# Eight loads at the end of a routed two-layer kernel: all at once, or two in flight

## The reference

```
x = x + gnn(layernorm(x), adj)
    agg = epsilon * x + adj @ x
    h   = silu(rmsnorm(agg @ W1 + b1) * rms_weight)      # 128 -> 512
    out = h @ W2 + b2                                    # 512 -> 128
x = x + ffn(layernorm(x))
    scores = x @ Wg.T + bg          # 8 experts, the best 2 per token
    p = softmax(top 2 scores)
    out = sum over the 2 experts of p * (relu(x @ W1[e].T + b1[e]) @ W2[e].T + b2[e])
```

## Time and profile before

| | |
|---|---|
| median of 3 runs | 562.39 us (561.38 to 563.0) |
| the profiled execution's own time | 561.8 us |
| its span | 560.0 us |
| TensorE busy | 531.0 us, 95% |
| VectorE, ScalarE, GpSimd busy | 64%, 53%, 73% |
| queue of SyncE (q1) | 104.08 MB, 51.1% of 16 engines' span |
| mean over the span | 219 GB/s |
| mean granted TensorE clock | 0.99 |

### The profile page before, as it was taken

The page is one execution under the profiler, slowest core; times in us unless marked ns, Lnnn a source line. Parts: engine busy times, 40 slices in busy tenths (PEclk is TensorE's granted clock), DMA queues, the critical chain, the costliest instruction groups (busy, mean ns, idle before and its releaser), DMA issues.

```text
span 560.0 us, 13703 instructions
## 1 busy us (share of the span) xinstructions
PE 531.0 (95%) x3642; PEld 440.8 (79%) x3642; DVE 357.9 (64%) x1202; ACT 296.5 (53%) x779; POOL 411.5 (73%) x671
## 2 busy tenths in 40 slices
PE   2999999999999999999999999999999999999982
PEld 1477766676666777567799999999999999999950
DVE  2558696886978969868867456654454444444483
ACT  3455654547645465554665455555555555555520
POOL 5423878788887878878877587888888766677770
PEclk9999999999999999999999999999999999999995
DMA  8998334553445543364165465677775747766998
GB/s 278 421 422 330 95 137 168 196 188 119 131 162 194 188 161 106 132 255 152 39 223 193 167 226 200 231 243 267 263 249 193 278 169 262 257 221 233 333 314 343
DMA packets 40203, 122.42 MB, mean 219 GB/s; under 512 B 7967, under 2 KB 18976, under 8 KB 37824
## 3 DMA queue, kind: packets, MB, share of 16 engines
q1 hardware_dynamic: 30768, 104.08, 51.1%
q0 software_dynamic: 8640, 16.93, 9.0%
q10 hardware_dynamic: 720, 0.54, 0.3%
HBM read 61.19 MB, written 24.02 MB: 152 GB/s over the span
## 4 chain that ended last, share of the span: by engine, by line
PE 63%; POOL 15%; issue 7%; DMA 5%; DVE 4%; ACT 4%; SPq 0%; DVEq 0%; POOLq 0%; ACTq 0%
PE ps_y L699 14%; PE ps_agg L589 8%; POOL slots L977 7%; PE ps_g L699 7%; PE ps_y L563 6%; POOL x_all L970 3%; PE ps_agg L668 3%; PE ps_h L668 3%; PE ps_h L672 3%; PE ps_agg L669 3%; PE ps_h L669 3%; PE ps_agg L672 3%; PE ps_t L576 3%; ACT hn L765 2%; PE ps_t L527 2%
## 5 line engine op out<-in xcount | busy, mean ns | idle before, releaser
L1045 POOL DMA_INDIRECT parts<-adj_in x142 | 141.5, 996 | 58.5 <-ACT adj_in L880 31.7
L977 POOL DMA_INDIRECT slots<-rows,dest x128 | 131.3, 1025 | 22.5 <-issue 22.0
L589 PE MATMUL ps_agg<-adj_in,xn_both 128*128 128x512 f32 x256 | 128.3, 610 | 10.1 <-DVE adj_in L1109 10.1
L880 ACT ACTIVATE adj_in<-adj_in,share 128x128 f32<-128x128 f32 x142 | 49.4, 395 | 101.1 <-issue 89.2
L699 PE MATMUL ps_y<-W2e,adj_in 128*128 x768 | 93.9, 275 | 0.0
L699 PEld LDWEIGHTS ps_y<-W2e,adj_in 128*128 128x128 f32 x768 | 89.9, 192 | 0.0
L1295 DVE TENSOR_TENSOR xe_split<-ps_t,xe_split 128x256 fp32r<-128x256 f32 x71 | 30.0, 424 | 80.3 <-ACT xe_split L828 74.8
L589 PEld LDWEIGHTS ps_agg<-adj_in,xn_both 128*128 128x128 f32 x256 | 45.1, 195 | 34.0 <-issue 31.1
L563 PEld LDWEIGHTS ps_y<-consts,siluT 128*128 128x128 f32 x480 | 57.0, 192 | 7.2 <-issue 7.2
L765 ACT ACTIVATE hn<-hb 128x512 f32<-128x512 f32 x64 | 39.7, 621 | 39.8 <-DVE hb L1115 39.8
L563 PE MATMUL ps_y<-consts,siluT 128*128 128x128 f32 x480 | 58.9, 277 | 0.0
(11 more groups left out here) (199 smaller groups left out, 1127.4 us busy)
## 6 DMA issues: line engine op xcount, KB each, us to landing
wcur<-expert_w SPq DMA_DIRECT2D x71, 512.0 KB
adj_in<-in_adjT SPq DMA_DIRECT2D x15, 2048.0 KB, 8.8
adj_in<-slots SPq DMA_DIRECT2D x71, 130.0 KB
expert_w<-parts SPq DMA_DIRECT2D x8, 512.0 KB, 5.2
out<-x_all SPq DMA_DIRECT2D x8, 512.0 KB, 8.0
x_all<-in_x SPq DMA_DIRECT2D x1, 3072.0 KB, 17.8
parts<-adj_in POOLq DMA_INDIRECT x142
adj_in<-in_adjT SPq DMA_DIRECT2D x2, 1024.0 KB, 7.6
```

Source lines behind the costliest of these rows:

```text
L589: ins = pe.matmul(ps_agg[par][:, :], xn[b % 2][:, m, :], adj_in[par][:, m, :], start=(m == 0), stop=(m == TPB - 1))
L880: ins = act.activation(ye[ku][:, j, :], yb[ku % 2][:, j, :], ACT.Copy, scale=share[ku][:, j:j + 1])
L977: pool.indirect_dma_start(out=slots, out_offset=bass.IndirectOffsetOnAxis(ap=dest[q % 2][:, c, j:j + 1], axis=0), in_=rows[q % 2][:, c, j, ...
L1045: pool.indirect_dma_start(out=parts, out_offset=bass.IndirectOffsetOnAxis(ap=goes[u % 8][:, j, :], axis=0), in_=ye[ku][:, j, :], in_offset ...
```

## The change

Before each low load from the third on, SyncE waits until the load two before has landed. The number of loads, their sizes, their destinations and their order are the same, and so is everything else in the kernel.

```
     GFIRST, FIRST = 11, 8
     EARLY = (2 * GTOK * GE - E * (TILE - 1)) // TILE
     BOTH_PAIRS = 24
+    IN_FLIGHT = 2
     CH = 8
...
             results_landed(counts[0])
             for n in range(NCH):
+                if n >= IN_FLIGHT:
+                    sp.wait_ge(s_low[n - IN_FLIGHT], 16)
                 sp.dma_start(low_part_in[n], parts_t[:, 0, n * CH:(n + 1) * CH, :]).then_inc(s_low[n], 16)
             for k in range(4):
                 sp.wait_ge(s_W1cur[k], 16 * ((NTILE + 3 - k) // 4))
```

## The result

The changed kernel takes 564.31 us (median of 16, 562.89 to 567.09); the kernel before, beside it, 561.63 (16 runs, 560.28 to 564.28). The ratio is 1.0047, with a 95% interval of 1.0032 to 1.0061: slower by 2.6 us. The forecast was 562.6, a change too small to be told from none; the range to 565.0 holds the time, but what came is the slower rival, which had a chance of 0.17.

A forecast was written before the change was run, and what follows sets the result against it. The bound was a chain of waits through the last scatter to high 4 to 7, with crowded transfers second. 0 us at a 3.7 us load, 0.2 at 3.8, put as +0.2: 562.6 on the median's scale, range 561.1 to 565.0.

The forecast's parts named there:

- slower rival: Low loads' round trips outlast SyncE's cover: +1.7 us at 4.3 us a load, +4.7 at 5.3; chance 0.17.
- odd chain 1, 3, 5, 7: SyncE's low loads: each odd one issues when the previous odd one lands; low 7 issues at 533.9, lands at 537.6.
- slack of 540:543: DMA engines at share 0.71, 185 GB/s before the change; high 3's 1.4 us of lateness was to fall into it.
- bytes of 527:533: DMA during throttled low loads: share forecast near 0.68 instead of 1.02.
- signs of being wrong: Low loads over 4 us, high 4 landing past 545 or issued past 541, or TensorE idle before 535.
- how long a load takes with at most one other ahead: Low loads two in flight: 3.7 us taken, between high 0's 3.6 and high 4's 3.8.
- rival's own rule: Three latencies chained to low 7: each 0.1 us on a load puts 0.3 us on high 3.
- low pair's 4.3 and 6.3: Latencies of low 0 and low 1 before the change, median 5.3; long latencies were called a queue, not a transfer's price.
- faster rival: Scatters land sooner in a lighter queue, so high 4 lands 1.3 us sooner: 561.1; chance 0.11.
- last gate: SyncE's wait before high 4 for the scatter issued at 534.45; taken to open at 540.4, unchanged by the edit.
- 1.6 us to spare: Low 7 was to land at 537.6, ahead of TensorE's start on its chunk at 539.16.
- 8.4 us of cover: SyncE's idle wait for scatters before high 0, until 533.53, meant to hide the added waits.

The follow-up runs named there:

- placebo: Changed kernel with its six waits moved to the expert biases' semaphore, long full, so none waits; ratio 1.000 (0.9981 to 1.0019) to the kernel before.

## Why the prediction was right or wrong

The place was right: the odd chain 1, 3, 5, 7 sets when SyncE is free, high 0 to 3 stand behind low 7, and high 4 lands right behind them. Right too: readers of the low parts of chunks 0 to 6 do not wait, the slack of 540:543 is filled, the bytes of 527:533 fell to 0.69 of 417 GB/s (forecast as a share, 0.68; the share itself read 0.93), and the waits as instructions cost nothing (placebo, 1.000). The prediction's signs of being wrong came, as it named them: low loads over 4 us, and high 4 landing past 545, at 519.9 + 27.0 = 546.9 on its clock.

The step that failed is "how long a load takes with at most one other ahead", 3.7 us. Counted from low 0:

| | forecast | changed kernel |
|---|---|---|
| low 1 lands | +6.6 | +5.8 |
| low 3 lands | +10.3 | +11.8 |
| low 5 lands | +14.0 | +15.9 |
| low 7 lands | +17.7 | +20.5 |
| high 0 issued | +14.5 | +16.5 |
| high 3 lands | +22.9 | +25.8 |
| high 4 lands | +24.3 | +27.0 |
| end of span | +40.3 | +42.1 |

Low 3, 5 and 7 took 6.0, 4.1 and 4.6 us, 14.7 for three against 11.1. Their 3.6 us, less the 0.8 by which low 1 came sooner, are the 2.8 us by which low 7 landed later than forecast. Every row below carries it on: 2.9 at high 3, 2.7 at high 4, 1.8 at the end. The rival's own rule, 0.3 us on high 3 for each 0.1 us on a load, held. At a mean of 4.9 and with low 1 as measured it gives high 3 at +5.8 + 14.7 + 5.2 = +25.7.

That the time lies inside the range is partly luck. The range held a load up to 4.6 us. For 4.9 the rival's rule gives +3.5 us, or 565.9 on the median's scale, and 564.3 came because two things outside the sum were favourable: low 1 landed 0.8 us sooner (0.2 and 0.6 in the two other profiles), and the stretch from high 4 to high 7 was shorter than before, as shown below.

Why 3.7 was the wrong row: high 0 and high 4 were each the first of a batch behind little or nothing. A load in a running pair always has a partner, and halving the bytes of both took 1.7 us off a round trip, not the 0.63 us that half a load is worth alone. The lower of the two rows was also a low reading: in three other profiles with the old ending high 0 took 3.9, 4.1 and 4.6 us, while high 4 took 3.8 or 3.9 each time. No row before has two loads in flight and nothing behind them. The low pair's 4.3 and 6.3 are nearest for the start, though six more loads stood behind them; I called their excess a queue and left 5.3 out of the range. The fit of the Trainium skill (DMA: Bandwidth & Descriptors, Anatomy of one DMA), 3.2 us, is further off still. The page gives it for a DMA that GpSimd issues, and has no term for others in flight; here no low load of full size took less than 3.5 us, even alone.

From the low loads alone the end should have moved by high 4's 2.6 us (+24.4 to +27.0). It moved by 2.0 in this profile, 1.5 to 2.0 in the two others (41.8 and 42.3 against 40.3). The difference arose between high 4 and high 7, the last load: 5.2 us before (544.3 to 549.5), 4.7 after (549.6 to 545.25 + 9.02 = 554.3). Before, 546:548 fell to 264 GB/s there; after, the stretch between high 5 and high 6 moved 317:

```profile
550.00:552.00 2.00, 0.47 (x2) 0.00 (x0) 1.97 (x3) 0.84 (x2) 0.00 (x0) 1.00 1.00 317
```

Behind high 7 nothing differs: the span ends 10.4 to 10.5 us after its landing in each of the ten profiles on the faster chips, the one-in-flight kernel included. So the end follows high 7. Why the stretch ahead of it varies is not shown: the placebo, with the old ending, has 4.5 us there.

The timed series give +2.6, +3.8 and +2.2 us, from the ratios 1.0047, 1.0068 and 1.0039. The 2.0 us of the ending lie inside the first and third interval and below the second (1.0042 to 1.0094). Whether something ahead of low 0 adds to the loss in some executions stays open; its issue scatters by more than the whole effect.

The faster rival's mechanism is there, and empty. SyncE no longer waited for scatters at the last gate. What kept high 4 until +21.1 was the late issue of high 0 to 3 and the 2.4 us of count reads behind them, which the prediction had left out; and the high loads ahead were late by more, so that high 4 had nothing to gain from going sooner.

A smaller miss: low 7 landed too late for TensorE, which waited 1.04 us for it; I had given it 1.6 us to spare. That cost nothing, since high 3 came later still.

## What to carry to other kernels

Before a queue is throttled, count the round trips that come to stand ahead of the next thing on the issuing engine, and set them against the wait that hides them: here three of 4 to 6 us against 8.4 us of cover were too many, one (four in flight) was free. Price a round trip from a row with as many loads in flight as there will be, not from the first of a batch. And where the end of a kernel is a packed run of transfers, bytes held back ahead of it cost time only as far as no slack in between takes them up. With waits to low 5 the profile moved 306 GB/s instead of 370 in the first 11.5 us, 381 instead of 318 in the next 10, and ended as before; with two in flight the slack was too small. Read GB/s there, not the busy share.

## What the runs showed that was not expected

- A 512 KB load from DRAM took 3.5 to 3.7 us with no other load in flight, from the fourth on and with or without scatters beside it; 4.3 to 4.5 with one partner and no scatters, 3.9 to 6.0 with a partner and scatters.
- The gate behind a scatter was open at least 1.9 us sooner when the low loads were throttled: by +11.8 instead of +13.7.
- Once the scatter no longer holds high 4, SyncE's own reads of four counts (2.4 us) stand between high 3 and high 4. A gate's bookkeeping is free only while the gate waits.
- The same kernel, before, takes 561.6 to 561.9 us (medians) elsewhere and 627.0 on one chip. In the profile of the kernel with waits to low 5 there, TensorE's granted clock is 0.98 and it is busy 88% of the span instead of 95%; most of the loss lies in the expert tiles, where TensorE, ScalarE and VectorE wait for each other. What slows them was not looked into.
- On one chip low 0 went between 517.7 and 523.2 us in four profiles, of kernels that do the same up to there: twice the effect that was to be measured.
